# Fusion convolutions of a MetaFormer block: 64 rows of each TensorE tile instead of 44, the added rows zero

## What is computed

```python
def cga_fusion(a, y, P):
    init = a + y
    ...
    pattn = jnp.broadcast_to(cattn + sattn, init.shape)
    gate = jax.nn.sigmoid(rconv(jnp.concatenate([init, pattn], 1), P['pg_w'], P['pg_b'], groups=C))
    out = init + gate * a + (1.0 - gate) * y
    return jnp.einsum('oc,bchw->bohw', P['op_w'], out) + P['op_b'][None, :, None, None]
```

## Time and profile before

| | |
|---|---|
| Median of 3 runs | 2606.95 us (2604.25 to 2609.1) |
| The profiled execution | 2610.89 us |
| Its span | 2609.1 us |
| Mean granted clock of TensorE | 0.886 |
| TensorE busy (matmuls) | 2270.9 us, 87% of the span |
| VectorE, ScalarE, POOL busy | 1429.2, 1152.3, 524.5 us |
| Moved by DMA | 434.57 MB, mean 167 GB/s |

### The profile page before, as it was taken

How to read it: one execution, slowest core, us unless ns; L and a number is a source line. 1 busy time by engine, 2 the same in 40 slices (tenths; PEclk the granted TensorE clock), 3 DMA queues, 4 the chain that set the end, 5 groups by cost and what they waited for, 6 DMA issues and landing times. The chain is left out here.

```text
span 2609.1 us, 69321 instructions
## 1 busy us (share of the span) xinstructions
PE 2270.9 (87%) x25034; PEld 1307.9 (50%) x25034; DVE 1429.2 (55%) x2562; ACT 1152.3 (44%) x2290; POOL 524.5 (20%) x903
## 2 busy tenths in 40 slices
PE   6679769889996999999699999999579999588887
PEld 3344437767862333333266666666245555233333
DVE  3345501111114777777577888888323333488887
ACT  4346432222224888888432332333011111377776
POOL 7610015102000000000256656656100000000000
PEclk9789869999997999999899999999755555799999
DMA  6999988776645777877466666666296663244443
GB/s 158 259 259 269 240 293 316 255 246 236 238 163 104 151 143 143 152 141 144 87 126 128 135 129 126 134 129 131 67 261 199 191 193 116 78 109 109 111 110 84
DMA packets 559393, 434.57 MB, mean 167 GB/s; under 512 B 363592, under 2 KB 498432, under 8 KB 555878
## 3 DMA queue, kind: packets, MB, share of 16 engines
q1 hardware_dynamic: 476982, 384.66, 56.4%
q10 hardware_dynamic: 76128, 22.48, 4.3%
q0 software_dynamic: 6128, 25.11, 3.8%
HBM read 247.30 MB, written 188.38 MB: 167 GB/s over the span
## 5 line engine op out<-in xcount | busy, mean ns | idle before, releaser
L615 PE MATMUL gate_ps<-gate_data,gate_wt 64*64 64x289 f32 x6144 | 391.9, 412 | 28.8 <-issue 21.1
L615 PEld LDWEIGHTS gate_ps<-gate_data,gate_wt 64*64 64x64 f32 x6144 | 304.8, 135 | 116.9 <-issue 45.4
L676 DVE TENSOR_TENSOR gate_out<-gate_gelu,gate_ps 128x578 f32<-128x578 f32 x96 | 72.2, 756 | 375.4 <-PE gate_ps L615 326.8
L968 ACT CAST mix_h<-mix_bank 96x512 f16<-96x512 f32 x512 | 267.5, 591 | 10.5 <-PE mix_bank L919 6.7
L2074 PE MATMUL fus_bank<-fus_xt,fus_taps 44*32 44x256 f32 x3840 | 211.5, 631 | 35.6 <-DMA fus_shift<-gate_shift 21.6
L653 ACT ACTIVATE gate_gelu<-gate_ps 128x578 f32<-128x578 f32 x96 | 62.8, 654 | 300.7 <-PE gate_ps L615 279.0
L2074 PEld LDWEIGHTS fus_bank<-fus_xt,fus_taps 44*32 44x32 f32 x3840 | 120.3, 172 | 120.9 <-issue 120.6
L1053 DVE TENSOR_SCALAR mix_hb<-mix_h,mix_b1q 96x1024 f16<-96x1024 f16 x256 | 122.8, 480 | 96.8 <-ACT mix_h L968 96.8
L919 PE MATMUL mix_bank<-mix_xq,mix_w1q 112*96 112x512 fp8e5 x512 | 142.9, 381 | 34.0 <-ACT mix_h L968 23.0
L1063 DVE CAST mix_hq<-mix_hb 96x2048 fp8e5<-96x2048 f16 x128 | 156.6, 1223 | 21.1 <-DVE mix_hb L1053 18.9
L255 PE MATMUL exp_y<-exp_win,exp_xb 48*128 48x192 f32 x1024 | 117.8, 369 | 48.7 <-ACT exp_out L292 28.1
(11 more groups left out here) (232 smaller groups left out, 4308.9 us busy)
## 6 DMA issues: line engine op xcount, KB each, us to landing
y<-exp_out SPq DMA_DIRECT2D x64, 816.0 KB, 12.1
gate_data<-y SPq DMA_DIRECT2D x24, 2176.0 KB, 19.0
g<-gate_out SPq DMA_DIRECT2D x48, 578.0 KB, 4.8
mix_sc<-g SPq DMA_DIRECT2D x31, 816.0 KB
wav_strips<-xp SPq DMA_DIRECT2D x96, 204.0 KB, 3.5
init<-wav_init SPq DMA_DIRECT2D x48, 272.0 KB, 2.3
fus_init<-init SPq DMA_DIRECT2D x48, 272.0 KB, 5.3
xp<-mix_xn SPq DMA_DIRECT2D x124, 102.0 KB, 2.8
```

The lines of the kernel that those rows point to most:

```text
L615: mm = pe.matmul(banks(a, v)[64 * g:64 * (g + 1), r], wt[q][64 * r:64 * (r + 1), 2 * a + g, n, :], src, start=n == 0, stop=n == 3)
L968: act.copy(h16[at.pair][:, m, h, :], bank[(2 * m + h) % len(bank)][0:HID, :]).then_inc(h16_ready, 1)
```

## The change

Each matmul of the fusion stage takes all 64 rows of its tile (`HALF = 64`). The 20 rows behind the 44 of data are zero in the weights and in the data: `clear` sets partitions 32 to 63 (on VectorE) and 96 to 127 (on GpSimd) of `taps`, `xt` and `spatial` to zero once, ahead of the loads, and the loads then fill partitions 0 to 43 and 64 to 107 as before. One semaphore `cleared` becomes one per slot for taps and lines, and one for the map; SP and ScalarE wait for them slot by slot, SP for the map in between. GpSimd waits for its own and VectorE's clears ahead of its loop, and its addition takes all 128 partitions.

```diff
@@ -1972,7 +1972,7 @@
     KF = 2 * REACH
-    KA = 64 + KF
+    HALF = 64
@@ -1989,10 +1989,11 @@
-        consts_in, cleared, own_done, map_done, gated, fused, step, added = (
-            k.sem(n) for n in ("consts_in", "cleared", "own_done", "map_done", "gated", "fused", "step", "added"))
+        consts_in, own_done, map_done, gated, fused, step, added = (
+            k.sem(n) for n in ("consts_in", "own_done", "map_done", "gated", "fused", "step", "added"))
         in_conv, in_pair, stored = ([k.sem(f"{n}{u}") for u in S] for n in ("in_conv", "in_pair", "stored"))
-        pe_turn = k.sem("pe_turn")
+        pe_turn, map_cleared = k.sem("pe_turn"), k.sem("map_cleared")
+        taps_cleared, lines_cleared = ([k.sem(f"{n}{u}") for u in S] for n in ("taps_cleared", "lines_cleared"))
@@ -2033,10 +2034,11 @@
-                sp.wait_ge(cleared, 1)
                 for u in S:
+                    sp.wait_ge(lines_cleared[u], 2)
                     load_lines(sp, 0, u, 0)
                     if u == 0:
+                        sp.wait_ge(map_cleared, 2)
                         for r in range(2):
                             sp.dma_start(spatial[64 * r:64 * r + KF].rearrange("p g b x -> p g (b x)"),
@@ -2069,7 +2071,7 @@
                             for r in range(2):
-                                rows = slice(64 * r, 64 * r + KF)
+                                rows = slice(HALF * r, HALF * (r + 1))
                                 for g in range(4):
@@ -2088,9 +2090,10 @@
-                act.wait_ge(cleared, 1)
                 for u in S:
+                    act.wait_ge(taps_cleared[u], 2)
                     load_taps(act, 0, u)
+                    act.wait_ge(lines_cleared[u], 2)
                     load_lines(act, 0, u, 1)
@@ -2115,20 +2118,29 @@
+            def clear(eng, rows):
+                for u in S:
+                    eng.memset(taps[u][rows], 0.0).then_inc(taps_cleared[u], 1)
+                    eng.memset(xt[u][rows], 0.0).then_inc(lines_cleared[u], 1)
+                    if u == 0:
+                        eng.memset(spatial[rows], 0.0).then_inc(map_cleared, 1)
+
             @block.gpsimd
             def _(pool):
+                clear(pool, slice(96, 128))
+                for u in S:
+                    pool.wait_ge(taps_cleared[u], 2)
+                    pool.wait_ge(lines_cleared[u], 2)
                 with pool.Fori(0, N) as i:
                     for u in S:
                         pool.wait_ge(in_conv[u], 96 * i + 96)
                         pool.wait_ge(gated, i * SLOTS + u + 1)
-                        pool.tensor_tensor(whole[u][0:KA], taps[u][0:KA, 2], taps[u][0:KA, 3], ALU.add).then_inc(added, 1)
+                        pool.tensor_tensor(whole[u][:, :, :], taps[u][:, 2], taps[u][:, 3], ALU.add).then_inc(added, 1)
 
             @block.vector
             def _(dve):
                 chain = Chain(dve, step, 3 * SLOTS)
-                for u in S:
-                    x = dve.memset(taps[u][32:64], 0.0)
-                x.then_inc(cleared, 1)
+                clear(dve, slice(32, 64))
                 dve.sem_inc(fused, SLOTS)
```

## The result

The changed kernel takes 2530.41 us (median of 4 runs, 2524.24 to 2547.39) against 2605.6 us (4 runs) for the one before: ratio 0.9721, 95% interval 0.9668 to 0.9774. That is 75 us less, where 103 were forecast. 2530 lies inside the range of 2465 to 2550. It lies outside the forecast's own bounds of 2478 to 2510, which are those for a clock that rose and DMA as the next bound; the range reached up to 2550 for the sake of the third rival.

A forecast was written before the change was run, and what follows sets the result against it. TensorE at clock 0.50 was taken to bound the fusion stage; at the upper clock DMA would, 103 us less, with clears and clock drops at nothing: 2606.95 - 103 = 2504 us, range 2465 to 2550.

The forecast's parts named there:

- third rival: Fusion stage: clock goes up and down, or TensorE isn't fed instructions at twice the rate; 76 us less, 2531 us, chance 0.10.
- The clock: Fusion matmuls: 64 rows, zeros counted, raise TensorE's granted clock from 0.50 to near 1.00, as 48 rows did in the wavelet.
- The first rival: Fusion stage: zeros don't count, or something else holds the clock at 0.50; no change, 2607 us, chance 0.11.
- TensorE at the upper clock: Fusion matmuls: 7.0 us a pair instead of 12.77, 184 us against 323 with pauses, 139 us less if nothing else were late.
- DMA as the next bound: Fusion stage's loads and stores: 63.01 MB at 270 GB/s need 233 us, so the stage ends 103 us earlier.
- The pauses of 16 us: TensorE in the fusion stage: some 16 us of pauses, mostly 2.7 us at each loop turn, kept in the sum unchanged.
- The drops of the clock: TensorE's gaps between pairs: drops cost 1.5 us each, hidden by 2.7 us of idle, so 0; up to 36 us uncovered.
- The clearing: VectorE's and POOL's clears ahead of the fusion loads: hidden, 0 us, bounds -1 and +1 us, 4 us if uncovered.
- first matmul within 1 us of 1902.7: Sign that the forecast is right: the fusion stage's first matmul starts about when it did before, despite the new clears.

The follow-up runs named there:

- e1: The changed kernel with its clears and semaphores, but fusion matmuls of 44 rows again instead of 64: 2615.22 us, ratio 1.0011 to the kernel before.
- e2: The changed kernel with 48 rows instead of 64 in the fusion matmuls, four of them zeros: 2536.79 us, ratio 0.9717 to the kernel before.
- e3: The changed kernel with the added 20 rows of lines and map set to 1.0 instead of 0.0, weights still zero: 2541.15 us, one run.
- e5: The kernel before the change (44 rows, its one clear) with two buffer slots instead of four: 2588.54 us, ratio 0.9912.
- e12: The changed kernel with two slots instead of four, base and init loaded for the first two pairs alone: 2453.09 us, one run.
- e4: The changed kernel with two buffer slots instead of four, so TensorE's loop body is half as long: 2501.53 us, ratio 0.9584 to the kernel before.
- e11: The changed kernel with two slots instead of four and the short loop body, run again on another chip: 2500.32 us, ratio 0.9569 to the kernel before.
- e9: The changed kernel with two slots, but TensorE's loop body holding two turns' work, 1920 instructions as with four slots: 2536.15 us, ratio 0.9695 to the kernel before.
- e10: The changed kernel with three buffer slots instead of four, a loop body of 92 KB: 2504.34 us, ratio 0.9587 to the kernel before.
- e7: The changed kernel, four slots, with two of the map convolution's five shifts, 192 matmuls a pair instead of 240: 2506.84 us, one run.

## Why the prediction was right, and what it missed

**The clock.** Right. "64 rows are more than the 48 that were enough, if a row of zeros counts": e1, e2 and e3 separate it. 44 rows 0.50, 48 rows 0.79 to 0.90, 64 rows 0.88 to 0.93 with zeros and 0.85 to 0.93 with ones (windows of 50 us from 1900 to 2150). Being busy alone did not raise it: e1 was busy 49.65 of 50 us and stayed at 0.50, and e5 was busy 50.00 of 50. How many rows a matmul uses matters as well, here at least. The first rival, the clock staying at 0.50, did not come about.

**TensorE at the upper clock.** Near enough: 7.0 us a pair from the wavelet's row, 7.0 in e12. That the two agree is in part chance: 240 matmuls without a wait take 6.5 us (2129.07 to 2135.58 in the changed kernel), and the rest in e12 is short waits between runs. The half of 12.77, 6.4, was closer; with DMA as the bound the difference counts for nothing.

**DMA as the next bound.** Right as a mechanism for a kernel that isn't held up otherwise: 270 GB/s taken, 301 measured in e4, 280 to 286 in e11; the bounds of the term, 263 GB/s (the expansion, DMA share 0.97) and 304 (63.01 MB in 207 us), held them. With the short body the kernel takes 2500 us where 2504 were forecast. For the change itself this step failed. "What is late next: DMA" was the wrong next. With the forecast, the last matmul would have ended some 220 us after the first (322.8 less 103); it was 251.8 in the change and 208.7 and 221.8 in the two-slot runs. The 30 to 43 us between are the instruction fetch, which the sum had at nothing beyond 16 us of pauses; e9 and e11, one body apart, differ by 25 us in this and by 36 us in the whole time. The fetch's pauses don't add to the DMA time in whole, since DMA works on while TensorE stands; but the loads for a slot aren't issued before its matmuls are done, so the pauses of TensorE become holes in DMA (0.82 instead of 0.92).

**The pauses of 16 us.** Here the error lay open in the rows: the earlier trace rows has a pause of 2.7 us at a turn, put down to ScalarE's gate. I carried it along as a fixed 16 us. It was the fetch (e5), two of the five pauses are put down to "issue" in the trace of before, and what is 16 us at one speed had to be looked at anew for twice the speed: it was 63. The third rival named it, "not fed instructions at twice the rate", with 0.10 for it and the clock's drops together, and its 2531 us is what came out. That is luck: its sum is of a clock at the upper level for a third of the time, and the clock was up most of the time (0.88 to 0.93). So is the range's holding 2530 with the forecast's mechanism incomplete.

**The drops of the clock.** Cost at nothing because TensorE had 2.7 us to spare in each pair. In the change it had nothing to spare. Its busy time from first to last matmul is 251.8 - 64.8 (waits) = 187 us, against 168.6 - 4.5 = 164 us in e12 at clock 1.00: some 23 us were lost to the lower level. In e4 it is 208.7 - 35.9 = 173 us. The sum is worked out from different kernels, not shown by a run of its own, but the trace of the change shows the drop behind a pause of the fetch. The 160 matmuls that take 4.6 us at the upper level took 7.46 here, and the clock of these 10 us was 0.66:

```profile
1992.29 7.46 PE L2076 MATMUL fus_bank<-fus_xt,fus_taps 64*32 64x256 f32 x160 [4.96 <-issue]
...
1990.00:2000.00 10.00, 7.71 (x177) 4.89 (x185) 4.04 (x4) 0.00 (x0) 0.52 (x1) 0.66 0.76 251
```

**The clearing.** Right. 2176 elements took 1.87 us on VectorE and 1.91 on POOL (2.0 reckoned). The rows below are the changed kernel's. From SP's first load (1885.0) to the first matmul (1897.7) it is 12.7 us, before 12.9. The sign "first matmul within 1 us of 1902.7" failed only since the whole stage began 5 us earlier in this execution; from the first clear to the first matmul it is 15.8 us, before 15.6.

```profile
L2124 POOL MEMSET fus_xt<- 32x2176 f32 x3 | 5.7, 1906 | 0.0
L2124 DVE MEMSET fus_xt<- 32x2176 f32 x3 | 5.6, 1872 | 1.2 <-issue 1.2
```

**What stays open.** How the rows in use and the clock hang together beyond the three counts that were run, and whether it is their number or its being a multiple of 16; whether a short body alone, with four slots kept, would give the kernel before what e5 gave; how much of a packet's time is its own and how much its wait among other queues; and how the gated convolution, which also fetches its instructions anew (52 packets from 400 to 770 us), would do with a shorter body. None was tried.

## What to carry to other kernels

When TensorE is busy and the granted clock stays at 0.50, look at how many rows its matmuls use, and try padding the contraction with zeros: it cost nothing here and was worth 75 us; 44 rows made 48 were enough. Before a loop on TensorE is unrolled over more buffers, count the bytes of its body against the bodies that the trace shows without instruction packets; two slots with a body that stays were worth some 36 us more than four, or two, with one that is fetched at each turn. A "<-issue" pause in the middle of a run without waits, 256 instructions after the last one, was the sign of it here.

## What the runs showed of the hardware

That the granted clock can stay at 0.50 under a TensorE that is busy 50.00 of 50 us (e5, 44 rows), and rises when rows of zeros are added (e2, 48 rows: 0.79 to 0.90 in the windows of 50 us).

That matmuls overlap by the profile: one of L2074 lasts 631 ns in the mean in the kernel before, and with 12.77 us for 240 one starts every 53 ns.

That TensorE can starve for instructions: at the upper clock and with DMA at 0.8 to 0.9 it stood for 63 us in all, up to 7.5 us at a time, where 256 instructions take 3.5 us to run (160 matmuls in 4.3 us). The packets are of 16 KB (0.87 MB in 53). By the estimate of 64 bytes an instruction, bodies of 61 KB (e4, 5 packets), 92 KB (e10, 6) and 98 KB (e7, 8) stayed, and bodies of 123 KB (the change, 53; e9, 48) did not. No run has a body between 98 and 123 KB.
